# Third-layer context mean and bias made once as eight rows and spread by identity rows, with the mean and the last stream sum moved in the order

## The reference

```
x = x + tanh(g_xattn[0]) * low-rank attention(norm(x), ctx);  x = x + tanh(g_ffn[0]) * mixture of 8 experts + shared
x = x + tanh(g_xattn[1]) * 16-head attention(norm(x), ctx);   x = x + tanh(g_ffn[1]) * mixture of 8 experts (layer 1)
x = x + tanh(g_xattn[2]) * (norm(x) @ W1.T + mean_k(ctx) @ W2.T + b)
x = x + tanh(g_ffn[2]) * fp4-quantised gated feed-forward(norm(x))
x = x + tanh(g_xattn[3]) * 16-head attention(norm(x), ctx);   x = x + tanh(g_ffn[3]) * mixture of 8 experts
```

## Time and profile before

| | |
|---|---|
| median of 3 runs | 748.66 us (747.25 to 750.33) |
| profiled execution, its own time | 748.58 us |
| its span | 746.8 us |
| mean granted clock of TensorE | 0.955 |
| busy: TensorE matmul, VectorE, ScalarE, GpSimd | 90%, 64%, 59%, 24% of the span |

### The profile page before, as it was taken

One profiled execution on the slowest core, in us unless ns is written; L12 is line 12 of the kernel. 1 busy time (PEld: TensorE's weight loads), 2 busy tenths in 40 slices (PEclk: granted clock), 3 DMA queues, 4 the chain that ended last, 5 costly groups with the idle time before them and its releaser, 6 DMA issues.

```text
span 746.8 us, 10207 instructions
## 1 busy us (share of the span) xinstructions
PE 673.7 (90%) x3566; PEld 487.5 (65%) x3575; DVE 476.5 (64%) x1093; ACT 437.3 (59%) x819; POOL 182.8 (24%) x215
## 2 busy tenths in 40 slices
PE   4889999998799898898999988998888997889997
PEld 1589996554467666676667676765554564767775
DVE  2467675585457467546554756467984763579996
ACT  4356454876556658557358475544226663887873
POOL 3414001630132051223332402032003001124521
PEclk9989999999899999999999999987999999799999
DMA  5112002020002000202020200010001000011000
GB/s 134 49 30 61 1 1 72 1 86 2 0 15 70 1 15 28 72 0 85 14 72 4 82 2 1 0 46 0 1 1 33 26 2 1 29 29 29 1 0 29
DMA packets 27361, 20.98 MB, mean 28 GB/s; under 512 B 5409, under 2 KB 22571, under 8 KB 27311
## 3 DMA queue, kind: packets, MB, share of 16 engines
q1 hardware_dynamic: 26591, 20.29, 9.2%
q10 hardware_dynamic: 720, 0.04, 0.1%
HBM read 19.80 MB, written 0.52 MB: 27 GB/s over the span
## 4 chain that ended last, share of the span: by engine, by line
PE 66%; DVE 18%; ACT 8%; issue 4%; POOL 2%; DMA 1%; ACTq 0%; DVEq 0%; POOLq 0%
PE PS L1457 58%; PE PS L1692 3%; PE PS L1563 2%; ACT XN L746 2%; DVE SN L1137 1%; PE PS L1714 1%; DVE H2l L1179 1%; PE PS L1614 1%; DVE H1l L1179 1%; ACT H1h L836 1%; DVE ST L1011 1%; DMA GW<-in_L_gate_T 1%; ACT PS L839 1%; PE PS L1478 1%; ACT G L839 1%
## 5 line engine op out<-in xcount | busy, mean ns | idle before, releaser
L642 POOL TENSOR_TENSOR WL<-RAW,WH 128x512 fp32r<-128x512 f32 (+2 forms) x76 | 89.2, 1190 | 155.1 <-ACT WH L730 154.8
L1179 DVE TENSOR_TENSOR H2l<-PS,H2h 128x512 fp32r<-128x512 f32 x72 | 48.9, 688 | 64.4 <-ACT PS L839 64.1
L634 POOL TENSOR_TENSOR RSTD<-VE,MHALF 128x4 f32<-128x4 f32 x18 | 18.7, 1039 | 205.1 <-DVE VE L1021 169.4
L1457 PE MATMUL PS<-H1h,WH 128*128 128x512 f32 x146 | 61.2, 419 | 6.9 <-DVE H1l L1179 6.9
L730 ACT ACTIVATE ATT<-PS 77x512 f32<-77x512 f32 (+5 forms) x92 | 45.8, 530 | 32.8 <-PE PS L1885 16.2
L1457 PE MATMUL PS<-XTh,WH 128*128 128x512 f32 x128 | 54.2, 423 | 11.2 <-DVE XTl L1039 5.7
L660 POOL TENSOR_TENSOR XT<-XT,YW 128x512 f32<-128x512 f32 x24 | 32.2, 1343 | 118.2 <-DVE YW L1116 118.2
L1457 PE MATMUL PS<-H1l,WH 128*128 128x512 f32 x146 | 58.6, 401 | 0.0
L1457 PE MATMUL PS<-H1h,WL 128*128 128x512 f32 x146 | 58.4, 400 | 0.0
L1259 DVE TENSOR_REDUCE MX<-PS 128x4 f32<-128x308 f32 x64 | 30.2, 473 | 38.2 <-PE PS L1457 38.2
L1457 PE MATMUL PS<-XTl,WH 128*128 128x512 f32 x128 | 53.4, 417 | 0.0
(11 more groups left out here) (251 smaller groups left out, 1685.8 us busy)
## 6 DMA issues: line engine op xcount, KB each, us to landing
RAW<-in_L_ffn_spec_W SPq DMA_DIRECT2D x4, 1024.0 KB, 5.6
RAW<-in_L_ffn_w SPq DMA_DIRECT2D x16, 256.0 KB, 3.1
RAW<-in_L_ffn_up_W SPq DMA_DIRECT2D x8, 256.0 KB, 2.7
RAW<-in_L_ffn_down_W SPq DMA_DIRECT2D x8, 256.0 KB, 3.6
RAW<-in_L_ffn_spec1a_W SPq DMA_DIRECT2D x2, 512.0 KB, 4.4
RAW<-in_L_ffn_spec1b_W SPq DMA_DIRECT2D x2, 512.0 KB, 5.6
RAW<-in_L_ffn_wg SPq DMA_DIRECT2D x4, 176.0 KB, 2.6
RAW<-in_L_ffn_wu SPq DMA_DIRECT2D x4, 176.0 KB, 2.7
```

The source lines that it names most:

```text
L634: step(g.tensor_tensor(RSTD[:, c], VE[:, c], MHALF[:, c], ALU.pow))
L642: g.tensor_tensor(lo, RAW[0:r["rows"], r["raw"] + s["c0"]:r["raw"] + s["c1"]], hi.bitcast(fp32), ALU.subtract).then_inc(lo_done, 1)
L1179: v.tensor_tensor(lo, full, hi.bitcast(fp32), ALU.subtract).then_inc(split_done, 1)
L1457: return t_.matmul(o, l, r, start=start, stop=stop)
```

## The change

The mean of the context is taken on VectorE at the start of `quantise_weights(0)`, inside the second layer's mixture, into CS (128 by 8). On TensorE, CS times W2A's lower half and ones times the bias give 8 rows, which ScalarE copies to CR, in G. `context_part` then spreads row t over the 128 tokens with a column of the identity that is read 128 times as the stationary operand (8 rows deep). The turn-back is split by halves with the context parts between, the first half's sum and statistics go ahead of BD3 on VectorE, and the keys' matmuls go behind the context parts. Four calls of `keep_clock` are added (4, 4, 4 and 6 matmuls). TensorE waits once more for the splits of the mixture, which are past by then.

```diff
-        CSB = ATT2[:, 0:T]
+        CR = G[0:B, 0, 0:D]
...
             mixture(1, 1)
 
+            act.wait_ge(cr_full, 1)
+            copy(CR, PS[3][0:B, 3 * D:4 * D]).then_inc(cr_ready, 1)
             for i in range(2):
                 act.wait_ge(k3_full, i + 1)
...
                 if i == 0:
+                    now(v.tensor_reduce(CS[:, :], CT[:, :].rearrange("p (b k) -> p b k", b=B), AX.X, ALU.add))
+                    v.tensor_scalar(CS[:, :], CS[:, :], 1.0 / KC, None, ALU.mult).then_inc(cs_ready, 1)
                     dve.wait_ge(in_w2, 16 * len(LAYER2))
...
+            summed(1)(0)
+            stats(5, 0, X)
             for m in range(3):
                 last = v.tensor_tensor(BD3[:, m, :]...
             last.then_inc(bd3_ready, 1)
-
-            now(v.tensor_reduce(CS[:, :], CT[:, :].rearrange("p (b k) -> p b k", b=B), AX.X, ALU.add))
-            v.tensor_scalar(CSB.rearrange("p (b s) -> p b s", b=B),
-                            CS[:, :].rearrange("p (b o) -> p b o", o=1).to_broadcast([128, B, S]), 1.0 / KC, None,
-                            ALU.mult).then_inc(csb_ready, 1)
-            norm(5, X, summed(1))
+            summed(1)(1)
+            stats(5, 1, X)
...
             pe.wait_ge(act_freed, LAST1["act"])
-            turn_back(1)
-
-            pe.wait_ge(bd3_ready, 1)
-            for i in range(2):
-                mm(PS[2 + i][:, 0:4 * KC], BD3[:, 1, :], CT[:, i * 4 * KC:(i + 1) * 4 * KC]).then_inc(k3_full, 1)
-
-            pe.wait_ge(csb_ready, 1)
+            pe.wait_ge(split_done, LAST1["hid"])
+            pe.wait_ge(cs_ready, 1)
             pe.wait_ge(in_w2, 16 * len(LAYER2))
+            mm(PS[3][0:B, 3 * D:4 * D], CS[:, :], W2A[:, D:2 * D], True, False)
+            mm(PS[3][0:B, 3 * D:4 * D], ones[:, 0:B], B2A[:, :], False, True).then_inc(cr_full, 1)
...
-            def context_part(some):
-                for t in some:
-                    mm(out2(t), CSB[:, t * S:(t + 1) * S], W2A[:, D:2 * D], t % TH == 0, False)
-                    mm(out2(t), ones[:, :], B2A[:, :], False, False)
+            def context_part(h):
+                for t in range(TH * h, TH * h + TH):
+                    mm(out2(t), ident[0:B, t:t + 1].to_broadcast([B, S]), CR, t % TH == 0, False)
...
-            context_part(range(0, 5))
+            keep_clock(4, PS[2])
+            turn_back(1, (0,))
+            pe.wait_ge(cr_ready, 1)
+            context_part(0)
+            turn_back(1, (1,))
+            context_part(1)
+            pe.wait_ge(bd3_ready, 1)
+            for i in range(2):
+                mm(PS[2 + i][:, 0:4 * KC], BD3[:, 1, :], CT[:, i * 4 * KC:(i + 1) * 4 * KC]).then_inc(k3_full, 1)
+            keep_clock(4)
             turn(4, *normed(5, XN), halves=(0,))
-            context_part(range(5, 8))
+            keep_clock(4)
             stream_part(0)
+            keep_clock(6)
             turn(4, *normed(5, XN), halves=(1,))
```

More of the change, by code:

```diff
@@ L476, in program @@
         max_done = sem("max_done")
-        csb_ready, a2_full = sem("csb_ready"), sem("a2_full")
+        cs_ready, cr_full, cr_ready, a2_full = sem("cs_ready"), sem("cr_full"), sem("cr_ready"), sem("a2_full")
         logit_full, dif_ready, gate_exp = sem("logit_full"), sem("dif_ready"), sem("gate_exp")
@@ L1643, in mixture, with turn_back @@
                             last.then_inc(down_full, 1)
-            def turn_back(n):
-                for b in range(B):
+            def turn_back(n, halves=range(2)):
+                for b in [TH * h + t for h in halves for t in range(TH)]:
                     if b % TH == 0:
```

## The result

The changed kernel took 745.04 us, the median of 6 runs (744.57 to 745.50), against 747.95 for the kernel before on the same chip (746.43 to 751.45, 6 runs): a ratio of 0.9954, 95% interval 0.9933 to 0.9975. The forecast was 745.3. The profiled execution took 745.11 us with a span of 743.4, against 748.58 and 746.8: 3.47 less, where the sum said 3.3. Mean granted clock 0.962 (0.955 before).

The account below looks back on a forecast made before the run. The stage between the second layer's mixture and the third's feed-forward was taken as bound by TensorE, largely at half clock. Gains of 3.65 and 0.1 less 0.45 made 3.3 us, from 748.58 to 745.3; range 743.5 to 748.0.

Parts of the forecast that it names:

- four thin passes: TensorE's passes over CS and ones that make the eight rows, from 492.00: 0.25 each, 1.0 us.
- Part 1: Mean ahead of the second layer's first weight quantisation: costs 0.45 us, bounds 0 and 1.0, mostly under GpSimd's port lock.
- Part 2: Eight rows, CR and spreading: 16 passes for 32, ending by about 497; first half's sum at 494.5.
- Part 3: Sum ahead of the key weights: BD3 at 497.4, key copies on ScalarE ending 499.25, ahead of the first half's normalising.
- Part 4: Third layer's stream passes: VectorE adds the halves at 503.05 and 506.65, 4.8 and 4.05 us earlier.
- Part 5: GpSimd's eight BDK tiles end at 506.55 and hold the next root: it gains 3.65 us, quantisation at 509.7.
- keep-clock run of 14: TensorE run before L1429 at 524.55: 3.2 us at full clock, closing a 0.38 gap; gain taken as 0.1.
- Rival B: All goes well: clock high, gap of 0.38 gone, moved mean free; 744.5, or 744.0 with earlier BDK tiles; chance 0.25.
- A: The forecast itself: GpSimd's BDK tiles set the gain; range 744.3 to 746.4; chance 0.50.
- Rival C: Clock falls in the change's thin work, low to about 505.5; quantisation gains 2.0; 747.0; chance 0.17.
- Rival D: Slower: clock low through the whole stage, keep-clock matmuls in the path; quantisation 2.1 later; 751.1; chance 0.08.
- line of 0.5%: Smallest change a measurement can tell, 3.7 us: lines 744.9 and 752.4; faster 0.39, within 0.55, slower 0.06.

Follow-up runs that it names:

- e4: The changed kernel with the context mean's two operations moved from the first weight quantisation to behind an H2l split of expert 2: 744.17 us, ratio 0.9951.
- e9: e7 with the context mean's two operations moved behind expert 0's first weighing in the second layer's mixture: 743.64 us, ratio 0.9942.
- e11: e9 with six more scalings of CS by 1.0 on VectorE beside the mean: 745.57 us, one run.
- e6: The changed kernel with GpSimd's eight BDK tiles split, five before the third mix's first root and three after it: 743.59 us, ratio 0.9941.
- e5: The changed kernel unaltered, run again in a second series: 743.41 us, ratio 0.9940 to the kernel before.
- e2: The changed kernel without its 18 added keep-clock matmuls: 743.38 us, ratio 0.9946 to the kernel before.
- e3: The changed kernel with its new order and keep-clock matmuls but the old context part of 32 passes over CSB and the bias: 751.06 us, ratio 1.0053.
- e1: The kernel before with only the eight rows and identity spreading, old order, no added keep-clock matmuls: 744.26 us, ratio 0.9957.
- e8: The changed kernel with e6's split, e7's order, e4's place for the mean, 3 keep-clock matmuls for 6, and 23 for 18 in the feed-forward: 742.62 us, ratio 0.9926.
- e10: e9 with two more scalings of CS by 1.0 on VectorE between the mean's reduce and its scaling: 740.98 us, one run.
- e12: e9 with e6's split of the key tiles on GpSimd, the version for use: 742.72 us, ratio 0.9927.
- e7: The changed kernel with the first half's turn-back ahead of the CS product and the first four keep-clock matmuls: 742.70 us, ratio 0.9928.

## Why the prediction was right

The mechanism came as forecast, in its main steps, and the total came out through terms of wrong size that cancel. The times in brackets are those of the prediction. They leave out the 0.45 of the mean, which its sum takes off at the end, while the measured ones hold the 0.24 by which T came later. So some agree better than they should; the point on the four thin passes compares them from T.

- **Part 1, the mean.** Forecast +0.45, with the reduce passing under GpSimd's held port. The gap between the two H1l grew from 3.99 to 4.40: 0.41. The new TENSOR_SCALAR ended at 314.45, the GpSimd operation at 314.42, and L1318 fell from 0.98 to 0.17, as described. The rule of the Trainium skill ("SBUF — State Buffer", section "SBUF: two separate sides") holds by these numbers; without it the term would have been 1.0. e4 and e9 to e11 show that the bound of 0 could have been had.
- **Part 2, eight rows.** 16 passes at 0.12: two groups of eight in 1.15 with their tails, ended by 497.09 (forecast 497). ScalarE's copy took 0.27 (bound 0.48). The first sum at 494.38 (494.5), though by another way: VectorE was to be free at 493.5 and wait a microsecond, but it started its weighing 0.33 late, was free at 494.12 and waited 0.26. The keep-clock matmuls in front were hidden by a delay that the prediction didn't know.
- **Part 3, the key copies in front of XN.** BD3 ended at 497.33 (497.4), the copies at 499.15 (499.25).
- **Part 4, the stream.** Adds at 503.02 and 506.60 (503.05, 506.65).
- **Part 5, GpSimd as the next bound.** Tiles from 501.07 to 506.39 (501.25, 506.55), root 506.49 (506.65), quantisation 509.56 (509.7). The gain there is 4.04 counted from T and 3.80 on the clock, as T came 0.24 later; forecast were 3.65, and 3.20 with the mean's cost. e6 is the test of the mechanism: with three tiles out of the way the root comes 1.05 earlier. One reading was wrong and cost nothing: the statistics, forecast for 505.4, were ready at 506.41, as the tiles stretched the two small operations at their end. The prediction knew that effect at 313 and did not count it here.
- **The four thin passes over CS and ones** were put at 0.25 each, 1.0 us, and took 0.62 (492.25 to 492.87). That brought the first sum 2.52 behind T in place of 2.88 (494.5 less 491.62), and everything behind it some 0.3 to 0.4 earlier: BD3's end 5.47 for 5.78, the adds 11.16 and 14.74 for 11.43 and 15.03, the tiles 9.21 for 9.63, the quantisation 17.70 for 18.08.
- **The other term that was mis-sized** is the 0.1 for the keep-clock run of 14. The prediction left open whether the run meets the full clock. It did: 13 in 3.19 in place of 4.66, two L1431 back to back, 0.46 gained. At 553 the clock took 0.67 back, of which the prediction said nothing, and some 0.2 went between the peak and the end. So 3.20 + 0.1 were forecast, and 3.80 + 0.46 - 0.67 - 0.2 = 3.4 measured: the mechanism was right, and the total also by errors that cancel. It is luck, too, that T stood so near in the two profiled executions (0.24 apart): in e5, the same kernel, it came 2.1 earlier.
- **Rival B** had the clock right (1.00 through the stage, the run in 3.2, the gap gone) and the mean wrong. The execution lies between A and B up to 551.5 and at A from 553 on.
- **Rival C** needed the clock to fall in the thin work. It does so without keep-clock matmuls (e2), from about 496 to 506. C's price is not tested by that: C had the quantisation gain 2.0 us with the keep-clock matmuls in the path at half clock, and e2, which has none of them, gains 3.28 from T. e2 does show why a slower TensorE costs little: its first add is 1.81 later than in after and its root only 0.76, since the tiles keep GpSimd until 14.16 behind T in any case.
- **Rival D** needed half clock through the whole stage. No profile shows that: with every pass of the old context part (e3) it is 1.00 up to 502 and again from 508.8 on, and with the keep-clock matmuls left out (e2) it is 1.00 from 508.8 on.
- By the line of 0.5%, the first series (0.9954) is no change and the second (e5: 0.9940) faster. The forecast put 0.55 and 0.39 on these two, and the measurement sits at the line between them. The median of the second series, 743.41, lies just below the range of 743.5 to 748.0.

## What to carry to other kernels

When a product has few different rows, make the rows once and spread them with a thin stationary operand: the passes halve in number and lose their costly alternation, and the gain was 3.36 us of 4.04 without any work on the clock. Reordering paid nothing by itself: with the old 32 passes it lost 0.34, with eight rows and a falling clock it stood level with the rows alone (18.46, 18.38), and only with the kept clock did it bring 0.68 more. After a stage has been cut, look at the engine that was "free" before; here GpSimd's block of eight tiles, 5.3 us long, took the path, and splitting it around the urgent operation was worth 0.66 us at the next stage.

## What the runs showed of the hardware

- Small VectorE operations are stretched beside GpSimd's: the 0.17 us TENSOR_SCALAR of L1022 and L1023 took 0.62 and 0.75 beside the BDK tiles, and 0.17 and 0.16 in e6, where GpSimd stood idle at that moment. In after that is 1.04 us of VectorE, hidden there behind the same tiles.
- TensorE's half-clock stretches come at different places in two executions of one kernel. From 20 to 32 us the clock was 1.00 in after and 0.59 in e5, the same kernel, as it was 1.00 in before and 0.57 in e1, whose instructions are the same up to 490. The 12 passes at the feed-forward's end took 1.60 in before, e1 to e3, e6 to e8 and e10 to e12, and 2.27 to 2.60 in after, e4, e5 and e9. The totals of low clock over the span go from 47 us (e6) to 86 us (e1). That this spreads the medians is not shown: in e5 the two slowest runs (745.16 and 745.58) had the highest clock (0.964), and in e7 the two slowest too (0.967).
- VectorE started an operation 0.33 us late with its signals up, or not, according to a few instructions that stood in its program 230 us earlier (e9, e10, e11). An edit far away can so move a stage by a third of a microsecond.
- Passes that alternate between a 128-row and a 1-row stationary operand start 0.21 us apart at a clock of 1.00 (e3: two pairs from 495.12 to 495.95), eight with 8 rows each 0.12 apart (after, 494.28), just as the stream's eight with 128 rows. The depth of the operand changes nothing here, the change of it does: in before the loads of the stationary operand start 0.11 apart within a pair of equal depth, whether 128 rows or 1, and 0.31 apart at each change.

```profile
495.62 0.30 PEld L1457 LDWEIGHTS PS<-W2A,ATT 128*128 128x128 f32 x2 [0.61 <-DVE ATT L1403]
...
496.04 0.29 PEld L1457 LDWEIGHTS PS<-B2A,ones 1*128 1x128 f32 x2
```

These are two such pairs: two loads 0.11 apart, 0.31 to the next pair, 0.42 in all.
